# Last MLP of a vision tower on one core: a third result buffer for the left-over tokens, their stores spread, and the rounding of the normalised values moved to GpSimd

## The chip, the cores and the metric

The kernel runs as one program on one core of one Trainium2 chip. The metric is the device time of one execution in microseconds. Before the change it was 2389.38 us, the median of three runs (2388.32 to 2389.45).

A core has five engines that run side by side and meet only at semaphores: TensorE (PE in the profile, with PEld for its weight loads), VectorE (DVE), ScalarE (ACT), GpSimd (POOL) and SyncE (SP), which here only issues transfers. Data lie in an on-chip memory of 128 partitions (SBUF); TensorE writes its products to a second one (PSUM).

## What is computed

A small vision transformer on 64 images. Patch embedding gives each image 197 tokens of 192 values; two attention layers and two MLPs follow, each behind a layer norm and with its input added. The change is in the last MLP, which is quantised:

```python
def _L1_ffn_ref(x0, w1, b1, alpha_w1, alpha_a1, w2, b2, alpha_w2, alpha_a2):
    QN, QP = (-8, 7)
    ...
    xq = _quant_act(x0, alpha_a1)        # round(clip(x / mean(alpha), -8, 7))
    wq1 = _quant_w(w1, alpha_w1)
    x1 = jnp.einsum('bsd,hd->bsh', xq, wq1)
    x1 = x1 * alpha_w1 * alpha_a1.mean() + b1
    x1 = jax.nn.gelu(x1, approximate=False)
    x1 = jnp.clip(x1, -10.0, 10.0)
    hq = _quant_act(x1, alpha_a2)
    wq2 = _quant_w(w2, alpha_w2)
    x2 = jnp.einsum('bsh,dh->bsd', hq, wq2)
    x2 = x2 * alpha_w2 * alpha_a2.mean() + b2
    return x2
...
    h = h + _L1_ffn_ref(_layernorm(h, axis=-1), ...)
```

Tokens are 192 wide, the hidden layer 768.

## The kernel before

Four stages follow each other: `embed_attend`, `mlp_0`, `attention_1`, `mlp_1`. The token stream `h` stays in SBUF all the time. Only `mlp_1`, the last, is changed; it takes about the last 205 of 2389 us.

Tokens are held in tiles of 128 rows. Two images (2 x 197 = 394 tokens) fill three tiles of 128 and leave ten tokens over; the ten tokens of all 32 pairs of images are gathered in three further tiles of 120, 120 and 80 rows. `mlp_1` works on groups of four tiles: 96 tiles make 24 groups, and a 25th group of the three left-over tiles is put in the middle, as group 12. A group is 512 tokens wide (the left-over group 320).

For a group g the steps are, with their lines:

- VectorE, `quantise` (line 1611): each tile is normalised from `h` to `z_xn` in float32 (line 1618), then the four tiles are rounded to `z_xq` in bfloat16 by adding and subtracting a large constant, in two instructions (line 1622). It signals `xn_made` and `quantised`.
- TensorE, `turn_x` (line 1745): transposes `z_xq` to PSUM, eight small products; signals `turned`.
- VectorE, `take_turned_x` (line 1628): clips the turned values to -8 and 7 and writes `z_xt`.
- TensorE, `up` (line 1758): six chunks of 128 hidden units, two products each, to four PSUM banks `z_bank_h`.
- ScalarE, `gelu` (line 1715): Gelu of each chunk to one of four buffers `z_act`.
- VectorE, `clip_chunk` (line 1636): limits each chunk in place.
- Rounding of the hidden values to `z_hid`: chunks 1 and 4 on GpSimd (line 1673), the others on ScalarE (line 1705), two chunks behind the Gelu.
- TensorE, `down` (lines 1769 to 1772): per tile eight products to `z_bank_y`.
- VectorE, `finish` (line 1646): scales the products from PSUM to `z_res`. It first waits (from the third group on) until the stores of the group two before, which used the same buffer of two, have landed.
- GpSimd, `add_stream` (line 1664): adds the token stream in place.
- SyncE, `store` (line 1688): stores the pieces of each tile. A pair of images has four such pieces, a group five or six; the left-over group has 32 pieces of ten rows (7.5 KB), since its rows belong to 32 images.

The order of work is written out by hand. Each engine walks through a list of steps by `in_turn`; a number beside a step says how many groups it is ahead of the loop counter. In one round g VectorE limits chunks 0 and 1 of group g+1, scales group g-1, limits chunk 2 of g+1, takes the turned x of g+2, limits chunks 3 to 5 of g+1 and normalises and rounds group g+3. GpSimd rounds chunk 1 of g+1, adds the stream of g-1 and rounds chunk 4 of g+1. TensorE does `up` of g+1, `turn_x` of g+2 and `down` of g.

## Time and profile before

| | us |
|---|---|
| median of three runs | 2389.38 |
| lowest, highest run | 2388.32, 2389.45 |
| the profiled execution, whole time | 2390.77 |
| its span, first to last instruction | 2389.0 |

The mean granted TensorE clock of the profiled execution is 0.988 of full speed. Over the whole span TensorE is busy 90% of the time, VectorE and ScalarE 84% each, GpSimd 72%. The last four of the forty slices of the page are those of the last MLP:

```profile
DVE  5776676888787689999998999989999998986997
ACT  4677776777776499999999999999999999996886
POOL 5777761333332489899989998989999998993544
```

A digit is the busy share of a fortieth of the span (60 us) in tenths. The page shows one execution; its durations are compared with its own span, and the 1.8 us between span and whole time lie outside.

### The profile page before, as it was taken

What the parts mean: (1) busy time and instruction counts of PE and PEld (TensorE: products, weight loads), DVE (VectorE), ACT (ScalarE), POOL (GpSimd) and SP (SyncE); (2) the same over time, 40 slices, a digit from 0 to 9 for tenths busy, and PEclk for the clock granted to TensorE, in tenths of its full rate; (3) what the DMA queues carried; (4) which work ended last, traced back from release to release, by engine and by line L of the source; (5) the groups of instructions that cost most, each with busy time, mean ns of one, the idle gap of its engine ahead of it and who ended that gap; (6) DMA issues with size and microseconds to landing.
All of it is one profiled execution on the core that took longest, in us unless ns stands there. A gap on an engine that the chain in (4) does not pass through costs nothing. (4 is left out here: it accounts for less than half of the span.)

```text
span 2389.0 us, 76378 instructions
## 1 busy us (share of the span) xinstructions
PE 2161.9 (90%) x25422; PEld 1699.0 (71%) x25422; DVE 1998.4 (84%) x4966; ACT 2008.5 (84%) x5695; POOL 1710.8 (72%) x2215
## 2 busy tenths in 40 slices
PE   5899999999999889999999999999999999988876
PEld 5788885888878567777777777777777777765554
DVE  5776676888787689999998999989999998986997
ACT  4677776777776499999999999999999999996886
POOL 5777761333332489899989998989999998993544
PEclk9999999999999999999999999999999999998999
DMA  6344420000100176666666666666666666673112
GB/s 187 100 115 113 120 71 28 6 5 5 44 15 5 30 124 120 124 121 121 118 125 118 126 118 120 119 124 119 126 119 120 121 122 121 123 120 51 57 48 60
DMA packets 734156, 222.65 MB, mean 93 GB/s; under 512 B 667590, under 2 KB 732720, under 8 KB 733808
## 3 DMA queue, kind: packets, MB, share of 16 engines
q1 hardware_dynamic: 733776, 221.36, 45.5%
q8 instruction: 41, 0.67, 0.1%
q14 instruction: 51, 0.42, 0.1%
q10 hardware_dynamic: 288, 0.20, 0.0%
HBM read 46.49 MB, written 9.68 MB: 24 GB/s over the span
## 5 line engine op out<-in xcount | busy, mean ns | idle before, releaser
L1516 POOL TENSOR_TENSOR b_pr<-b_pr,fc 128x394 f32<-128x394 f32 (+1 forms) x768 | 652.4, 870 | 123.6 <-DVE fc L1436 123.6
L1365 ACT ACTIVATE b_pr<-b_scores,fc 128x197 f32<-128x197 f32 (+1 forms) x1536 | 632.1, 440 | 2.6 <-issue 1.6
L1501 POOL TENSOR_TENSOR b_halves<-b_pr,b_halves 128x394 f16<-128x394 f32 (+1 forms) x640 | 565.3, 909 | 31.5 <-ACT b_halves L1334 27.3
L1273 PE MATMUL b_banks<-fp,wqkv 128*128 128x197 f16 x3840 | 378.8, 249 | 42.4 <-DVE b_qk L1420 38.7
L1430 DVE TENSOR_REDUCE fc<-b_scores 128x2 f32<-128x394 f32 x768 | 395.6, 556 | 4.0 <-PE b_scores L1291 1.9
L1273 PEld LDWEIGHTS b_banks<-fp,wqkv 128*128 128x128 f16 x3840 | 320.8, 98 | 83.7 <-DVE b_qk L1420 61.1
L1334 ACT ACTIVATE b_halves<-b_pr 128x788 f16<-128x788 f32 x384 | 342.6, 892 | 4.9 <-POOL b_pr L1516 4.9
L1365 ACT ACTIVATION_READ_ACCUMULATOR b_pr<-b_scores,fc 128x1 f32 (+1 forms) x1536 | 340.5, 222 | 0.0
L977 POOL TENSOR_TENSOR h<-h,fp_bias 69x192 f32 (+3 forms) x128 | 133.4, 1070 | 266.8 <-DVE m_xn L139 266.8
L1420 DVE SCALAR_TENSOR_TENSOR b_qk<-b_banks,b_qk 128x394 f16<-128x394 f32 x384 | 214.7, 559 | 101.5 <-ACT b_qk L1348 101.3
L1280 PE MATMUL b_banks<-wqkv,fp 128*128 128x384 f16 (+1 forms) x1280 | 254.7, 330 | 40.8 <-DVE h L1455 38.8
L1291 PE MATMUL b_scores<-b_qk 64*128 64x197 f16 (+1 forms) x4608 | 265.3, 248 | 4.6 <-ACT b_pr L1365 4.5
L479 PE MATMUL tokens<-tok_w,parts 128*128 128x192 f16 (+1 forms) x2304 | 212.0, 254 | 49.8 <-POOL parts L338 49.8
L479 PEld LDWEIGHTS tokens<-tok_w,parts 128*128 128x128 f16 (+1 forms) x2304 | 198.2, 109 | 60.0 <-POOL parts L338 39.6
L1291 PEld LDWEIGHTS b_scores<-b_qk 64*128 64x128 f16 (+1 forms) x4608 | 182.8, 103 | 64.6 <-issue 32.0
L338 POOL TENSOR_TENSOR parts<-patches,parts 128x394 f16<-128x394 f32 x192 | 178.9, 961 | 54.0 <-ACT parts L381 53.9
L1280 PEld LDWEIGHTS b_banks<-wqkv,fp 128*128 128x128 f16 (+1 forms) x1280 | 113.9, 105 | 127.2 <-DVE h L1455 53.1
L1348 ACT ACTIVATE b_qk<-b_banks 128x394 f16<-128x394 f32 x384 | 192.2, 519 | 11.1 <-PE b_banks L1273 7.2
L1077 PE MATMUL m_bank_y<-fp,m_hid 128*128 128x192 f16 (+1 forms) x2304 | 195.4, 246 | 1.3 <-DVE h L955 1.3
L1077 PEld LDWEIGHTS m_bank_y<-fp,m_hid 128*128 128x128 f16 (+1 forms) x2304 | 190.4, 105 | 1.7 <-issue 1.5
L1025 ACT ACTIVATE m_act<-m_bank_h,fc_bias 128x394 f32<-128x394 f32 x192 | 112.8, 588 | 87.1 <-PE m_bank_h L1066 75.2
L1066 PE MATMUL m_bank_h<-m_xt,fc 128*128 128x394 f16 x960 | 165.6, 329 | 2.1 <-DVE m_xt L945 2.1
(252 smaller groups left out, 4371.2 us busy)
## 6 DMA issues: line engine op xcount, KB each, us to landing
patches<-in_x SPq DMA_DIRECT2D x64, 588.0 KB, 4.4
b_pt<-b_halves SPq DMA_TRANSPOSE x384, 3.1
out<-z_res SPq DMA_DIRECT2D x62, 96.0 KB
fc<-b_halves SPq DMA_TRANSPOSE x192, 3.2
fp<-b_halves SPq DMA_TRANSPOSE x192, 3.2
m_raw_weights<-in_wqkv SPq DMA_DIRECT2D x2, 1152.0 KB, 6.8
out<-z_res SPq DMA_DIRECT2D x32, 51.8 KB
h<-h SPq DMA_DIRECT2D x32, 44.2 KB
```

What stands on the lines that cost most here:

```text
L479: last = t.matmul(tokens[m][0:ROWS[c], c * D:(c + 1) * D], parts[m][:, pa, k, COLS[c]], tok_w[:, pb, k, :], start=(k == 0 and n == 0), sto ...
L1077: last = t.matmul(bank_y[m][0:ROWS[c], c * D:(c + 1) * D], hid[b][:, pa, f, lo:lo + ROWS[c]], S["fp"][:, pb, f, :], start=(f == 0 and j == ...
L1273: last = t.matmul(out[:, g * SEQ:(g + 1) * SEQ], w[:, (2 * n + g) * P:(2 * n + g + 1) * P], x, start=(j == 0), stop=(j == 4))
L1280: last = t.matmul(out[0:ROWS[c], 0:VH], x[:, COLS[c]], w[:, col:col + VH], start=(j == 0), stop=(j == 4))
L1291: last = t.matmul(scores[n % 2][0:ROWS[c], e, c * SEQ:(c + 1) * SEQ], qk[rows, n, pa, 0, COLS[c]], qk[rows, n, pb, 1, :], start=(j == 0), ...
L1334: return nc.scalar.activation(dst, src, ACT.Copy)
L1348: nc.scalar.activation(qk[:, n, 0], banks[:, k, 0:2 * SEQ].rearrange("p (g t) -> p g t", g=2), ACT.Copy, scale=QK_SCALE).then_inc(qk_hi, 1)
L1365: last = nc.scalar.activation(pr[n % 3][0:ROWS[c], c, e, :], scores[n % 2][0:ROWS[c], e, c * SEQ:(c + 1) * SEQ], ACT.Exp, bias=nmx[n % 2][ ...
L1420: v.scalar_tensor_tensor(out=qk[:, n, 1], in0=banks[:, k, 0:2 * SEQ].rearrange("p (g t) -> p g t", g=2), scalar=QK_SCALE, in1=qk[:, n, 0], ...
L1430: v.reduce_max(nmx[n % 2][:, :, e], scores[n % 2][:, e, 0:2 * SEQ].rearrange("p (c t) -> p c t", c=2), AX.X, negate=True).then_inc(max_mad ...
L1501: nc.gpsimd.tensor_tensor(halves[n % 3][0:ROWS[c], c, 1, :, 0:SEQ], pr[n % 3][0:ROWS[c], c], halves[n % 3][0:ROWS[c], c, 0, :, 0:SEQ], ALU ...
L1516: last = nc.gpsimd.tensor_tensor(p, p, inv, ALU.mult)
```

## The change

- The left-over group (`LEFT`, group 12) gets a third buffer `z_res2` of its own. `finish` and `add_stream` use it for that group, and `finish` of that group waits for no store. The semaphores of the two other buffers no longer count its stores.
- SyncE no longer stores the left-over group at its turn. After the stores of each later group it issues four of the 32 pieces; after eight groups all are out. A wait for them stands before the last waits.
- The rounding to `z_xq` is taken from VectorE and given to GpSimd as a new step `quantise`, the last of its round, for group g+3. It waits for `xn_made` and for the transposes of two groups before, and signals `quantised`. VectorE's own `quantise` now ends with the normalising, and still waits for `quantised` of two groups before.

```diff
@@ -1528,8 +1528,11 @@
     tiles = [(p, k) for p in range(n_img // 2) for k in range(3)]
     groups = [tiles[k:k + GROUP] for k in range(0, len(tiles), GROUP)]
     assert all(len(g) == GROUP for g in groups) and len(rows_left) < GROUP
-    groups.insert(len(groups) // 2, [("left", k) for k in range(len(rows_left))])
+    LEFT = len(groups) // 2
+    groups.insert(LEFT, [("left", k) for k in range(len(rows_left))])
     count = len(groups)
+    LEFT_STORES = 4
+    assert LEFT_STORES * (count - 1 - LEFT) >= n_img // 2
 
     def rows(tile):
         return rows_left[tile[1]] if tile[0] == "left" else P
@@ -1562,7 +1565,7 @@
 
     def stores(last):
 
-        return 16 * sum(len(pieces(tile)) for g in range(last % 2, last + 1, 2) for tile in groups[g])
+        return 16 * sum(len(pieces(tile)) for g in range(last % 2, last + 1, 2) if g != LEFT for tile in groups[g])
 
     with ExitStack() as ctx:
         sb, ps, sem = stage_tools(nc, ctx)
@@ -1572,11 +1575,12 @@
         act_out = [sb(f"z_act{r}", [P, WIDE]) for r in range(4)]
         hid = [sb(f"z_hid{b}", [P, HC, WIDE]) for b in range(2)]
         low_half = [hid[b][:].rearrange("p f t -> p (f t)").bitcast(F16).rearrange("p (f t h) -> p f t h", f=HC, h=2)[:, :, :, 0] for b in range(2)]
-        res = [sb(f"z_res{b}", [P, GROUP, D]) for b in range(2)]
+        res = [sb(f"z_res{b}", [P, GROUP, D]) for b in range(3)]
         bank_x = ps("z_bank_x", [KH, 2, WIDE], BF16)
         bank_h = [ps(f"z_bank_h{r}", [P, 512]) for r in range(4)]
         bank_y = ps("z_bank_y", [P, 2, 512])
         stored = [sem(f"z_stored{b}") for b in range(2)]
+        left_stored = sem("z_left_stored")
         (xn_made, quantised, turned, xt_done, fc_made, gelu_made, clipped, done_by_s, done_by_p, made_y, scaled, h_done, scaled_rstd) = map(sem, (
             "z_xn_made", "z_quantised", "z_turned", "z_xt_done", "z_fc_made", "z_gelu_made", "z_clipped", "z_done_by_s", "z_done_by_p",
             "z_made_y", "z_scaled", "z_h_done", "z_scaled_rstd"))
@@ -1617,10 +1621,6 @@
                         r, j = rows(tile), column(tile)
                         last = v.tensor_scalar(xn[b][0:r, k, :], tokens(tile), mean[0:r, j:j + 1], rstd[0:r, j:j + 1], ALU.subtract, ALU.mult)
                     last.then_inc(xn_made, 1)
-                    dve.wait_ge(xn_made, g + 1)
-                    for lo, hi, r in halves(g):
-                        last = v.tensor_scalar(xq[b][0:r, lo:hi, :], xn[b][0:r, lo:hi, :], ROUND, -ROUND, ALU.add, ALU.add)
-                    last.then_inc(quantised, 1)
 
                 def take_turned_x(g):
                     n = starts(g)[-1]
@@ -1636,9 +1636,9 @@
                     v.tensor_scalar(a, a, S["q_hi"][:, 0:1], S["q_lo"][:, 0:1], ALU.min, ALU.max).then_inc(clipped, 1)
 
                 def finish(g):
-                    b = g % 2
+                    b = 2 if g == LEFT else g % 2
                     dve.wait_ge(made_y, g + 1)
-                    if g >= 2:
+                    if g >= 2 and g != LEFT:
                         dve.wait_ge(stored[b], stores(g - 2))
                     for lo, hi, r in halves(g):
                         scale = S["q2_scale"][0:r, :].unsqueeze(1).to_broadcast([r, hi - lo, D])
@@ -1653,7 +1653,7 @@
                 slots = h[:].rearrange("p i c d -> p (i c) d")
 
                 def add_stream(g):
-                    b = g % 2
+                    b = 2 if g == LEFT else g % 2
                     pool.wait_ge(scaled, g + 1)
                     for lo, hi, r in halves(g):
                         x, at = res[b][0:r, lo:hi, :], [column(tile) for tile in groups[g][lo:hi]]
@@ -1674,20 +1674,34 @@
                                                 ROUND + float(LOW_BITS), ALU.mult, ALU.add).then_inc(done_by_p, 1)
                     return make
 
-                in_turn([(round_chunk(ON_POOL[0]), 1), (add_stream, -1), (round_chunk(ON_POOL[1]), 1)])
+                def quantise(g):
+                    b = g % 2
+                    pool.wait_ge(xn_made, g + 1)
+                    if g >= 2:
+                        pool.wait_ge(turned, g - 1)
+                    for lo, hi, r in halves(g):
+                        last = nc.gpsimd.tensor_scalar(xq[b][0:r, lo:hi, :], xn[b][0:r, lo:hi, :], ROUND, -ROUND, ALU.add, ALU.add)
+                    last.then_inc(quantised, 1)
+
+                in_turn([(round_chunk(ON_POOL[0]), 1), (add_stream, -1), (round_chunk(ON_POOL[1]), 1), (quantise, 3)])
 
             @block.sync
             def _(sp):
+                left = [(k, piece) for k, tile in enumerate(groups[LEFT]) for piece in pieces(tile)]
+
                 def store(g):
-                    b = g % 2
                     sp.wait_ge(h_done, g + 1)
                     for k, tile in enumerate(groups[g]):
                         for i, lo, hi, row in pieces(tile):
-                            if g == count - 1 and k % 2:
+                            if g == LEFT or (g == count - 1 and k % 2):
                                 continue
-                            sp.dma_start(out[i, lo:hi, :], res[b][row:row + hi - lo, k, :]).then_inc(stored[b], 16)
+                            sp.dma_start(out[i, lo:hi, :], res[g % 2][row:row + hi - lo, k, :]).then_inc(stored[g % 2], 16)
+                    if g > LEFT:
+                        for k, (i, lo, hi, row) in left[LEFT_STORES * (g - LEFT - 1):LEFT_STORES * (g - LEFT)]:
+                            sp.dma_start(out[i, lo:hi, :], res[2][row:row + hi - lo, k, :]).then_inc(left_stored, 16)
 
                 in_turn([(store, 0)])
+                sp.wait_ge(left_stored, 16 * len(left))
                 for g in (count - 2, count - 1):
                     sp.wait_ge(stored[g % 2], stores(g))
 
```

## Rows read from the trace of the kernel before

**Rows 1.** Stretches of the last MLP: busy us and (instructions), clock, DMA share, GB/s.

```profile
core 0: us, PE busy (x) PEld busy (x) DVE busy (x) ACT busy (x) POOL busy (x), PEclk, DMA share, GB/s
2206.30:2264.20 57.90, 47.64 (x416) 33.39 (x416) 57.63 (x121) 52.54 (x81) 31.87 (x32) 1.00 0.17 54
...
2298.70:2325.50 26.80, 20.47 (x159) 14.77 (x156) 21.73 (x47) 20.27 (x32) 11.76 (x12) 0.87 0.17 52
```

**Rows 2.** Timeline of VectorE in one group: start us, us, what, count.

```profile
2250.67 0.54 DVE L1636 TENSOR_SCALAR z_act<-z_act,singles 128x512 f32<-128x512 f32 x1
2251.12 0.68 DVE L1628 TENSOR_SCALAR z_xt<-z_bank_x 96x1024 bf16<-96x1024 bf16 x1
2251.73 2.23 DVE L1636 TENSOR_SCALAR z_act<-z_act,singles 128x512 f32<-128x512 f32 x3
2253.88 1.61 DVE L1618 TENSOR_SCALAR z_xn<-h,mean,rstd 128x192 f32<-128x192 f32 x4
2255.53 0.63 DVE L1622 TENSOR_SCALAR z_xq<-z_xn 128x384 bf16<-128x384 f32 x2
2256.07 1.00 DVE L1636 TENSOR_SCALAR z_act<-z_act,singles 128x512 f32<-128x512 f32 x2
2256.99 1.01 DVE L1646 TENSOR_TENSOR z_res<-z_bank_y,q_scale 128x384 f32<-128x384 f32 x2
```

**Rows 3.** Timeline of the other engines in the same group, idle time before in brackets.

```profile
2250.84 2.38 POOL L1664 TENSOR_TENSOR z_res<-h,z_res 128x384 f32<-128x384 f32 x2 [0.23 <-DVE z_res L1646]
2250.90 0.24 PE L1769 MATMUL z_bank_y<-q_sum,base 128*128 128x192 f16 x1 [1.29 <-DVE z_res L1646]
2250.98 0.66 PE L1771 MATMUL z_bank_y<-q,z_hid 128*128 128x192 f16 x6
...
2253.60 0.92 POOL L1673 TENSOR_SCALAR z_hid<-z_act,singles 128x512 f32<-128x512 f32 x1 [0.38 <-DVE z_act L1636]
...
2254.17 1.45 ACT L1715 ACTIVATE z_act<-z_bank_h,q_bias,q_scale 128x512 f32<-128x512 f32 x2 [0.68 <-PE z_bank_h L1758]
...
2256.21 0.65 PE L1745 MATMUL z_bank_x<-ident_b,z_xq 128*96 128x128 bf16 x8
...
2257.16 0.69 POOL L1673 TENSOR_SCALAR z_hid<-z_act,singles 128x512 f32<-128x512 f32 x1 [2.64 <-DVE z_act L1636]
```

**Rows 4.** Single instructions by line: duration ns min/median/max; GpSimd's last addition (timeline).

```profile
L1636 DVE TENSOR_SCALAR z_act<-z_act,singles x2: 636/930/1223, 2251.7 to 2252.3; 128x512 f32<-128x512 f32 x2
L1618 DVE TENSOR_SCALAR z_xn<-h,mean,rstd x1: 751/751/751, 2253.9 to 2253.9; 128x192 f32<-128x192 f32 x1
L1618 DVE TENSOR_SCALAR z_xn<-h,mean,rstd x2: 361/364/367, 2254.6 to 2254.8; 128x192 f32<-128x192 f32 x2
L1673 POOL TENSOR_SCALAR z_hid<-z_act,singles x50: 534/694/958, 2193.4 to 2372.0; 128x512 f32<-128x512 f32 x48, 128x320 f32<-128x320 f32 x2
2377.93 1.94 POOL L1664 TENSOR_TENSOR z_res<-h,z_res 128x384 f32<-128x384 f32 x2 [2.05 <-DVE z_res L1646]
```

**Rows 5.** SyncE's stores behind the left-over group (duration ns), and the stall.

```profile
L1688 SPq DMA_DIRECT2D out<-z_res x35: 289/329/1189, 2294.9 to 2308.9; - x35
2310.42 1.17 PE L1771 MATMUL z_bank_y<-q,z_hid 128*128 128x192 f16 x6
2316.03 1.45 ACT L1715 ACTIVATE z_act<-z_bank_h,q_bias,q_scale 128x512 f32<-128x512 f32 x2 [3.37 <-PE z_bank_h L1758]
2309.14 1.02 DVE L1646 TENSOR_TENSOR z_res<-z_bank_y,q_scale 128x384 f32<-128x384 f32 x2 [3.16 <-DMA out<-z_res]
```

**Rows 6.** Timeline of VectorE, the scaling of groups 0, 8, 13, 16 and 21.

```profile
2206.29 1.01 DVE L1646 TENSOR_TENSOR z_res<-z_bank_y,q_scale 128x384 f32<-128x384 f32 x2
...
2264.22 1.01 DVE L1646 TENSOR_TENSOR z_res<-z_bank_y,q_scale 128x384 f32<-128x384 f32 x2
...
2298.67 1.01 DVE L1646 TENSOR_TENSOR z_res<-z_bank_y,q_scale 128x384 f32<-128x384 f32 x2
...
2325.47 1.01 DVE L1646 TENSOR_TENSOR z_res<-z_bank_y,q_scale 128x384 f32<-128x384 f32 x2
...
2361.69 1.01 DVE L1646 TENSOR_TENSOR z_res<-z_bank_y,q_scale 128x384 f32<-128x384 f32 x2
```

## The prediction, made before the change was timed

> **What bounds the kernel now.** Read the table of stretches first [rows 1]. From 2206.3 to 2264.2 us of the span, inside the last MLP, VectorE (DVE) is busy 57.63 of 57.90 us, ScalarE (ACT) 52.54, GpSimd (POOL) 31.87: VectorE sets the pace and ScalarE is next. Eight groups of four tiles pass here, so ScalarE needs 52.54/8 = 6.57 us a group. The starts of VectorE's scaling (`finish`) give the period: (2264.22 - 2206.29)/8 = 7.24 us [rows 6]. The second row, 2298.7 to 2325.5, is another stage altogether: VectorE is busy only 21.73 of 26.80 us and the granted TensorE clock falls to 0.87. That is the stall behind the left-over group.
>
> Then read one group on VectorE in the timeline [rows 2]. There is no gap between its instructions; each starts some 0.09 us before the record of the one in front ends. The order is the kernel's: limit chunks 0 and 1, scale, limit chunk 2, take the turned x, limit 3, 4 and 5, normalise four tiles, round them (0.63 us for two instructions at L1622). The same group on the other engines [rows 3]: GpSimd works 2.38 us on the addition and 0.92 and 0.69 us on its two roundings; ScalarE waits 0.68 us for TensorE once a group.
>
> Then compare single durations [rows 4]. The same `z_act` instruction takes 0.636, then 1.223 us, where a pair of them that meets nothing takes 1.00 us; the first `z_xn` takes 0.751, the next two 0.36 to 0.37. The slow ones are those that meet GpSimd: `z_act` number two runs against the addition, the first `z_xn` against the rounding at 2253.60. GpSimd in turn needs 0.92 for a rounding that takes 0.69 when VectorE is scaling from PSUM. So VectorE's limiting, normalising and rounding and any GpSimd instruction exclude each other, while scaling and the taking of x (both read PSUM) are not touched. This is the point on which the change turns.
>
> **The left-over group's stores.** Its 120+120+80 rows leave in 32 stores of ten rows. From the end of its addition SyncE issues 35 stores in the 14 us before 2309.15 [rows 5], and the scaling two groups later, in the same buffer, waits 3.16 us for the last of them. ScalarE then stands 3.37 us and TensorE's six matmuls take 1.17 us where 0.66 is normal (granted clock 0.87 over the stretch). Price of it all: from the scaling at 2298.67 to that at 2325.47 three periods pass [rows 6]: 26.80 - 3 x 7.24 = 5.1 us. With a third buffer nobody waits for these stores. What becomes late next? SyncE: after the change a group after the middle issues its own 5 or 6 stores and 4 more, ten of about 0.35 us, 3.5 us in a period of 7. The scaling of a group waits for the stores of two groups before; these start right after their addition and have a whole period and more to land, and the left-over stores stand behind them in the queue, never in front of the same group's. If SyncE needed the 14/35 = 0.4 us for each, ten would still be 4 us. I cost the new stores at nothing and take back all 5.1 us. The eight groups that take four stores each end with group 20, so nothing is added at the end.
>
> **Rounding of x: what VectorE gives away.** Take t = 0 at the end of normalising (2253.88 + 1.61 = 2255.49) [rows 2]. Before: rounding to t = 0.67, chunks 0 and 1 limited by 1.58, scaling 1.50 to 2.51, chunk 2 limited by 2.96 (one period after 2250.67 + 0.54). Without the rounding the limiting starts at -0.09 in place of 0.58: 0.67 us less. Were that all, VectorE would need 6.57 us, exactly what ScalarE needs; nothing below 6.57 is to be had.
>
> **What GpSimd takes on.** Two instructions a group, 128x384 float32 to bfloat16, two constants. The trace has no such one. The nearest is its own TENSOR_SCALAR at L1673: 0.534 us for 320 columns, 0.69 for 512 undisturbed [rows 4, 3]. On the line between them 384 columns take 0.534 + 64 x 0.158/192 = 0.59 us; I call it q and take 0.59. The bounds are the two rows themselves, 0.534 and 0.692; a 16-bit output is not known to cost more. The other bound, far off, is the addition of the same width, 1.94 us for two undisturbed [rows 4], 0.97 each.
>
> Now the collision. GpSimd can start 0.09 us after VectorE ends (2257.07 to 2257.16 [rows 2, 3]), so the first rounding asks at t = 0.1, when the limiting of chunk 0 already runs (-0.09 to 0.45). The rows show what a pair in this order costs: the GpSimd rounding at 2253.60 found chunk 5 running until 2253.96 and ended at 2254.52, 0.56 later, that is its own 0.69 less 0.13; the normalising behind it ended 0.11 after that, and a limiting, 0.17 longer, would end 0.28 after. So:
> chunk 0 limited at 0.45; first rounding ends 0.45 + 0.59 - 0.13 = 0.91; chunk 1 limited 0.91 + 0.28 = 1.19 (0.91 if undisturbed, from 0.45 + 0.46); second rounding ends 1.19 + 0.46 = 1.65; meanwhile VectorE scales from PSUM, undisturbed, 1.10 to 2.12; GpSimd's rounding of chunk 1 follows its second one, to 1.65 + 0.69 = 2.34; chunk 2, ready at 2.03, ends 2.34 + 0.28 = 2.62. Before it ended at 2.96. From there on the order of both engines is as before: the addition starts behind chunk 2 in either kernel. So the period is 7.24 - (2.96 - 2.62) = 6.90 us. In general chunk 2 ends at 0.45 + 2 x (q - 0.13) + 0.28 + 0.69 + 0.28 = 1.44 + 2q, and the period is 5.72 + 2q: 6.79 at q = 0.534, 7.10 at 0.692.
>
> The Trainium skill, SBUF — State Buffer, section Who interferes with whom, says that the pair of ports that VectorE and GpSimd share is an exclusive lock, held for the whole instruction by whoever issues first. By that the order in the sum above (chunk 0, first rounding, chunk 1) follows from the order of issue, as in the trace; the same section wants the conflict put off the critical path, which this change does not do, VectorE being the path.
>
> **Who waits for the moved step.** TensorE's turning needs the second rounding: 1.65 + 0.08 + 0.65 = 2.38. The products `down` behind it start at 2.25 at the earliest anyway (end of scaling plus 0.13); 0.13 us later costs nothing while ScalarE has slack. From the start of `down` to the first Gelu are 2254.17 - 2250.90 = 3.27 us [rows 3]: the Gelu comes at 5.65 in place of 5.92, period 6.90, so ScalarE has 0.33 us left of its 0.68. VectorE takes the turned x at 2.53, after 2.38. GpSimd's new wait for `xn_made` stands in front of the next group's rounding of chunk 1, whose input is there only at 1.19; the wait for `turned` is a period old. GpSimd then has 3.4 + 0.69 + 1.2 us of work in 6.9. All of this is hidden, with 0.15 us as the smallest cover (turning against taking).
>
> **Where it is not hidden.** At the start nothing else runs: 0.09 + 2 x 0.59 in place of 0.63 delays the first turning by 0.6 us. At the end the 0.13 us of `down` may show; 0.2 us. Together 0.8.
>
> **Sum.** The 25 groups are rounded in turn; three in the run-up, one before the first scaling, so 21 periods, 2206.29 to 2361.69 [rows 6], have a moved rounding: 21 x 0.34 = 7.1 us. With the stall 5.1 + 7.1 - 0.8 = 11.4 us. The profiled execution took 2390.8 (span 2389.0 and 1.8 around it), so it would be 2379.4; the median of the runs is 1.4 lower, 2389.4, and gives **2378.0 us**. In formula: 2385.1 + 21 x (period - 7.24).
>
> **Rivals.**
> 1. The roundings hardly meet VectorE (they slip in where it reads PSUM, or the lock is short). For it: conflicts before cost 0.1 to 0.7 us, not always the whole instruction. Against: chunks 0 and 1 stand right behind normalising. Period 6.57 to 6.75: 2371.0 to 2374.8.
> 2. q is longer than the line gives, 0.70 to 0.85 us, or there is one more conflict: period 7.12 to 7.42, 2382.6 to 2388.9. The move alone pays only below q = 0.76 (5.72 + 2q = 7.24); at that point 2385.1, the stall's share alone. For it: 0.92 us is seen for a disturbed 512 columns; against: there the wait is counted in.
> 3. Slower than before: GpSimd's rounding costs as much as its addition of the same width, 0.97 us. Period 7.66, 21 x 0.42 = 8.8 more: 2393.9, and 2395 with the turning then late (0.45 + 0.84 + 0.28 + 0.84 = 2.41, turned at 3.14). It decides from q = 0.86, where 21 periods eat the 4.3 us of stall and start. Against it: 0.69 us for 512 columns of the same operation. The Trainium skill, GPSIMD Engine Reference, section 3.1 Elementwise, speaks for it: for ordinary elementwise work VectorE stays the rule, and two inputs cost 2.6 cycles an element at 1.2 GHz. As an estimate from that page 384 columns would be 0.83 us and the time 2388; its best case of 1.8 cycles gives 0.58, and the row at 512 columns is on the side of the latter.
> 4. The stall does not go (a store in front of the scaling is still late): 2378.0 + 5.1 = 2383.1. Against it the half-empty queue above.
>
> **How the numbers follow.** Forecast 0.52 (own range 2375.7 to 2382.2 from the two rows for q), rival 1 0.15, rival 2 0.20, rival 3 0.07, rival 4 0.06. The range takes the forecast, rival 4, most of rival 2 and the upper part of rival 1: 2372.5 to 2386.5. A difference of 0.2%, 4.8 us, is about what a measurement can tell here: faster is under 2384.6. Faster: 0.52 + 0.15 + 0.06 and a third of rival 2, 0.79; slower 0.06; the rest, 0.15, within.
>
> **What the profile would show.** VectorE: no 0.63 us of `z_xq`; the two `z_act` behind `z_xn` no longer 1.00 but near 1.28 us; scaling every 6.9 us. GpSimd: a new group of 50, mean above 0.6 with its waits. No wait of `z_res` for a DMA, TensorE's clock 1.00 over the middle. ScalarE's wait for `z_bank_h` near 0.3 us. I would be wrong if q is beyond 0.76, if VectorE waits for the turning (a gap in front of `z_xt`), or if scaling too suffers from GpSimd.

## The result

The changed kernel took 2424.84 us (median of four runs, 2420.43 to 2429.58) against 2389.41 us for the kernel before. The ratio is 1.0146, 95% interval 1.0123 to 1.0169: 1.5% slower, where 0.5% faster was forecast. The time lies outside the range and beyond all four rivals.

Page of the profile after, parts 1 and 4 (busy us by engine; the chain that ended last, share of the span):

```profile
PE 2180.9 (90%) x25422; PEld 1712.9 (71%) x25422; DVE 1993.8 (82%) x4916; ACT 2009.2 (83%) x5695; POOL 1789.0 (74%) x2265
...
POOL 6%; issue 2%; DVE 1%; PE 1%; ACT 0%; POOLq 0%; ACTq 0%; DVEq 0%
POOL z_xq L1683 3%; POOL z_res L1664 2%; POOL z_hid L1673 1%; DVE z_xn L1622 0%; DVE z_act L1636 0%; PE z_bank_h L1772 0%; PE z_bank_x L1759 0%; DVE z_xt L1628 0%; PE z_bank_y L1785 0%; ACT z_hid L1719 0%; ACT z_act L1729 0%; POOLq L1606 0%; DVE z_res L1646 0%; DVE rstd L757 0%; PE z_bank_y L1783 0%
```

GpSimd is 78 us busier than in [rows 1]'s kernel as a whole (1710.8 before, 1789.0 now), and it stands first in the chain, with the moved rounding as the largest line. The moved instruction itself, in the view of its line (duration ns min/median/max, 50 of them):

```profile
L1683 POOL TENSOR_SCALAR z_xq<-z_xn x50: 850/1612/2056, 2187.6 to 2388.7; 128x384 bf16<-128x384 f32 x48, 120x384 bf16<-120x384 f32 x1, 80x192 bf16<-80x192 f32 x1
```

A median of 1.61 us. The prediction's q was 0.59 and its bounds 0.53 and 0.69. The 21 periods between the scaling of group 0 and that of group 21, as one stretch of after; the answers to it in before are [rows 1, 6]:

```profile
2212.90:2387.90 175.00, 137.97 (x1083) 99.12 (x1082) 145.46 (x274) 138.63 (x212) 143.68 (x126) 0.91 0.15 47
```

175.0 us in place of 2361.69 - 2206.29 = 155.4, and VectorE (third busy number) now idles 29.5 us of it, where in [rows 1] it had no gap. The whole difference of the two spans, 29.3 us, is made up so: 19.6 in these periods; 7.5 in the run-up (from VectorE's reciprocal of the norm to the first scaling 2212.85 - 2183.74 = 29.1 us, before 2206.29 - 2184.67 = 21.6); 3.1 at the end (2418.3 - 2387.9 against 2389.0 - 2361.7); less 0.9, by which this execution came to the reciprocal earlier.

**Where a group's time goes now.** The chain of waits of after over one group (start us, us, what; "issue" is time without a wait that the profile shows):

```profile
2235.77 3.19 POOL z_xq L1683 x2
2238.96 0.68 POOL z_hid L1673
2239.64 2.11 POOL z_res L1664 x2
2241.74 0.33 issue
2242.07 0.02 POOLq L1681
2242.09 0.04 issue
2242.13 0.91 POOL z_hid L1673
2243.04 1.02 issue
2244.07 0.02 POOLq L1672
2244.08 0.03 issue
```

Every piece of work is GpSimd's: 3.19 for the two roundings of x, 0.68 for chunk 1, 2.11 for the addition, 0.39 until chunk 4 is limited, 0.91 to round it, 1.07 until the normalising is through. That closes in 8.34 us, since the next rounding of x starts at 2244.11, and the next round closes in 8.47, at 2252.58; VectorE's scalings follow in turns of 7.07 and 9.73 us, which is the same mean, 8.40. The 0.39 and 1.07 are waits for VectorE, but VectorE's limiting and normalising there stand behind GpSimd's own instructions ([rows 2 to 4] show the same 0.38 and the first `z_xn` of 0.751), so they belong to the loop. Before, GpSimd had 2.64 us to spare in front of chunk 1 [rows 3]. VectorE and TensorE wait on this loop: TensorE's turning 2.65 us, VectorE's taking 1.45. VectorE and GpSimd thus meet not only at semaphores, as the section on the chip has it: each also lengthens instructions of the other.

```profile
2239.01 0.65 PE L1759 MATMUL z_bank_x<-ident_b,z_xq 128*96 128x128 bf16 x8 [2.65 <-POOL z_xq L1683]
2239.70 0.69 DVE L1628 TENSOR_SCALAR z_xt<-z_bank_x 96x1024 bf16<-96x1024 bf16 x1 [1.45 <-PE z_bank_x L1759]
```

**The run-up.** Stretches of after, four us each from 2188 (columns as in [rows 1]), and the turning of group 0:

```profile
2188.00:2192.00 4.00, 1.20 (x12) 0.68 (x11) 0.65 (x2) 0.00 (x0) 2.61 (x2) 0.99 0.00 0
2192.00:2196.00 4.00, 3.91 (x10) 1.43 (x11) 2.85 (x8) 2.68 (x4) 2.73 (x2) 0.50 0.02 4
...
2190.66 0.65 PE L1759 MATMUL z_bank_x<-ident_b,z_xq 128*96 128x128 bf16 x8 [2.61 <-POOL z_xq L1683]
```

TensorE stands idle for 2.61 us in front of the first turning, and the clock granted falls to 0.50, the lower of its two levels, 1.2 in place of 2.4 GHz, and stays there until about 2208. Before it was 1.00 there; one stretch of that kernel:

```profile
2192.00:2196.00 4.00, 2.80 (x20) 1.43 (x19) 3.79 (x8) 4.00 (x8) 0.70 (x1) 1.00 0.02 4
```

### The profile page after: what moved, and what is told of

Its sections match the earlier page's. It is cut to its first block and busy times, and to the rows that moved or that the text cites. A ratio compares the mean times of both kernels' runs of the same rounds, so it can differ in the third digit from the quotient of the medians.

```text
span 2418.3 us, 76401 instructions
## 1 busy us (share of the span) xinstructions
PE 2180.9 (90%) x25422; PEld 1712.9 (71%) x25422; DVE 1993.8 (82%) x4916; ACT 2009.2 (83%) x5695; POOL 1789.0 (74%) x2265
```

## The experiments

The reasons on trial were these. What makes the moved instruction 1.5 us long (the type written, the operation, or waiting for VectorE)? Is the rest of the prediction's model right once q is? How much is the stores' part worth? How much of the loss is TensorE's clock? The kernel before took 2389 to 2395 us in the different comparisons, so ratios are compared and not medians. The 21 periods are those of one profiled execution each.

| run | ratio to before, 95% interval | 21 periods, us (before 155.4) |
|---|---|---|
| both parts (the change) | 1.0146 (1.0123 to 1.0169) | 175.0 |
| 1, stores only | 0.9986 (0.9977 to 0.9995) | 151.9 |
| 12, stores only, TensorE kept busy | 0.9981 (0.9972 to 0.9990) | 150.2 |
| 2, rounding only | 1.0132 (1.0116 to 1.0147) | 176.7 |
| 3, both, GpSimd writes float32 | 1.0124 (1.0109 to 1.0140) | 175.0 |
| 7, both, TensorE kept busy | 1.0113 (1.0097 to 1.0128) | 173.4 |
| 6, both, step of one addition | 1.0083 (1.0067 to 1.0098) | 167.2 |
| 5, both, multiply by a pointer, add | 0.9991 (0.9981 to 1.0000) | 153.7 |
| 9, both, one pass, multiplier from a pointer | 0.9994 (0.9985 to 1.0003) | 152.7 |
| 8, both, one pass, constants | 0.9952 (0.9939 to 0.9966) | 143.4 |
| 11, the same, TensorE kept busy | 0.9938 (0.9926 to 0.9950) | 142.0 |

Runs 4 and 10 were executed once each, 2435.5 us (with its added stage) and 2383.2 us, and serve for their traces. A pointer in the table is an operand that GpSimd reads from SBUF, one value for each partition, in place of a constant in the instruction.

**1. The stores alone.** The hunks of the change on `LEFT`, `z_res` and `store`, without those on `quantise`.

> Only the stores' part of the change: third buffer for the left-over group, its 32 stores spread, the rounding of x stays on VectorE. Theory of the prediction (the stall is 5.1 us and goes whole): 2384.3 us, 0.2% faster than before, period 7.24 us throughout, no wait of z_res for a DMA. Rival (the spread stores hold something else up, or the stall only moves): 2387 to 2390 us, with a wait of z_res or a longer period in the groups behind the middle.

The wait for a DMA is gone and the periods behind the middle are 7.24 us; the 21 periods are 3.5 us shorter than before, not 5.1. The ratio says 0.14%, 3.3 us, between the 0.2% of the theory and the rival's nothing. The missing part lies just ahead of the left-over group's scaling, in two periods that are 1.6 us longer than without the fall (8.03 and 7.47 us against 6.69 and 7.23 in run 12), where the clock falls (columns as in [rows 1]):

```profile
2276.00:2280.00 4.00, 3.06 (x27) 1.78 (x24) 3.97 (x11) 3.59 (x8) 1.17 (x3) 1.00 0.30 94
2280.00:2284.00 4.00, 3.23 (x23) 3.11 (x24) 4.00 (x9) 2.56 (x5) 3.15 (x4) 0.64 0.04 12
```

The kernel before had 1.00 in the four microseconds from 2280 to 2284 of its own profile. The profiled execution was the slowest of the eleven (2388.66 us, the median is 2386.39), so how often the clock falls there isn't known.

**2. The rounding alone.** The hunks on `quantise` and the order of GpSimd, without the stores.

> Only the rounding of x moved to GpSimd; the left-over stores as before. Theory 1 (all of the loss is the moved rounding, and at a period of 8.4 us the scaling two groups behind the left-over one comes 16.8 us later, after its stores have landed some 14 us behind the addition): about 2425 us, as with both parts, no or hardly any DMA wait of z_res. Rival (the stall adds to it): 2430 us. If the moved rounding were innocent and the stores to blame: 2385 or less.

2420.5 us: the rounding alone carries the loss. I had expected hardly any DMA wait, and there is one of 2.37 us, yet the two periods around it are 17.6 us where two usually are 16.8: the stall costs 0.8 us in so slow a loop.

```profile
2321.49 1.02 DVE L1642 TENSOR_TENSOR z_res<-z_bank_y,q_scale 128x384 f32<-128x384 f32 x2
2330.97 1.02 DVE L1642 TENSOR_TENSOR z_res<-z_bank_y,q_scale 128x384 f32<-128x384 f32 x2 [2.37 <-DMA out<-z_res]
2339.13 1.01 DVE L1642 TENSOR_TENSOR z_res<-z_bank_y,q_scale 128x384 f32<-128x384 f32 x2
```

**3. GpSimd writes float32.**

```diff
-        xq = [sb(f"z_xq{b}", [P, GROUP, D], BF16) for b in range(2)]
+        xr = [sb(f"z_xr{b}", [P, GROUP, D]) for b in range(2)]
+        xq = [xr[b][:].rearrange("p k d -> p (k d)").bitcast(BF16).rearrange("p (k d h) -> p k d h", k=GROUP, h=2)[:, :, :, 1] for b in range(2)]
...
-                        last = nc.gpsimd.tensor_scalar(xq[b][0:r, lo:hi, :], xn[b][0:r, lo:hi, :], ROUND, -ROUND, ALU.add, ALU.add)
+                        last = nc.gpsimd.tensor_scalar(xr[b][0:r, lo:hi, :], xn[b][0:r, lo:hi, :], ROUND, -ROUND, ALU.add, ALU.add)
```

> Both parts of the change, but GpSimd writes the rounded x as float32, and TensorE reads the upper 16 bits of each value, which are the same bfloat16. One thing differs: the type that GpSimd writes. Theory W (the 1.6 us of a rounding is the price of writing 16 bits): a rounding takes 0.6 to 0.65 us, the period is 5.72 + 2q = 6.9 to 7.0 us, the time 2378 to 2380 us. Rival O (the price is that of the operation, two additions of constants, or of its two immediate operands): a rounding still takes 1.5 to 1.6 us and the time is 2420 to 2430 us. Rival L (the price is the waiting for VectorE): the same, 2420 or more.

The median stayed at 1.61 us, the 21 periods at 175.0 and the ratio, 1.0124, within the noise of 1.0146. The type is innocent.

**4. Each form by itself.** Ahead of the last MLP, on tiles that are free then, GpSimd alone, every instruction waited for; three rounds of 13 forms.

```diff
+                for _ in range(3):
+                    then(e.tensor_scalar(o[:, 0:2, :], a[:, 0:2, :], ROUND, -ROUND, ALU.add, ALU.add))
+                    then(e.tensor_scalar(f[:, 0:2, :], a[:, 0:2, :], ROUND, -ROUND, ALU.add, ALU.add))
+                    then(e.tensor_scalar(f[:, 0:2, :], a[:, 0:2, :], s, ROUND, ALU.mult, ALU.add))
+                    then(e.tensor_scalar(o[:, 0:2, :], a[:, 0:2, :], s, ROUND, ALU.mult, ALU.add))
+                    then(e.tensor_scalar(f[:, 0:2, :], a[:, 0:2, :], 2.0, ROUND, ALU.mult, ALU.add))
+                    then(e.tensor_scalar(f[:, 0:2, :], a[:, 0:2, :], ROUND, None, ALU.add))
+                    then(e.tensor_scalar(o[:, 0:2, :], a[:, 0:2, :], ROUND, None, ALU.add))
...
```

> The kernel with the stores' part alone, and before the last MLP a stage in which GpSimd works alone, with all other engines idle: each form of instruction three times, one after another. Theory W: every form that writes bfloat16 (128x384) takes about 1.5 us and every one that writes float32 about 0.6, whatever the operations. Rival O: add and add of two constants takes 1.5 us with either output, multiply by a pointer and add a constant 0.6 with either. Rival L (waiting for VectorE): all forms take 0.6 us, since VectorE is idle. The time of the whole is longer by the stage, 40 to 60 us.

Groups by line, in the order of the diff (L1615 to L1621), then the 512-wide pair L1624 (multiply by pointer, add) and L1625 (add, add); busy us and mean ns of one:

```profile
L1625 POOL TENSOR_SCALAR z_hid<-z_hid 128x512 f32<-128x512 f32 x3 | 5.8, 1932 | 0.2
L1615 POOL TENSOR_SCALAR z_xq<-z_xn 128x384 bf16<-128x384 f32 x3 | 4.5, 1499 | 0.3
L1616 POOL TENSOR_SCALAR z_xn<-z_xn 128x384 f32<-128x384 f32 x3 | 4.5, 1494 | 0.2
L1620 POOL TENSOR_SCALAR z_xn<-z_xn 128x384 f32<-128x384 f32 x3 | 3.5, 1173 | 0.3
L1621 POOL TENSOR_SCALAR z_xq<-z_xn 128x384 bf16<-128x384 f32 x3 | 3.5, 1168 | 0.2
...
L1624 POOL TENSOR_SCALAR z_hid<-z_hid,singles 128x512 f32<-128x512 f32 x3 | 2.1, 692 | 0.3
L1617 POOL TENSOR_SCALAR z_xn<-z_xn,singles 128x384 f32<-128x384 f32 x3 | 1.8, 587 | 0.3
L1618 POOL TENSOR_SCALAR z_xq<-z_xn,singles 128x384 bf16<-128x384 f32 x3 | 1.8, 587 | 0.3
L1619 POOL TENSOR_SCALAR z_xn<-z_xn 128x384 f32<-128x384 f32 x3 | 1.5, 512 | 0.3
```

This settles it for rival O. Add and add takes 1.49 us, with either output; multiply and add takes 0.51 with constants and 0.59 with a pointer; a single addition takes 1.17, twice the pair with a multiplication. The same at 512 columns: 1.93 against 0.69. Nothing else ran, so it isn't waiting; 0.1 us of the 1.61 in the kernel is. Other pairs, an addition of a pointer among them, were not tried, so why an addition in first place is slow stays open.

**5 and 6. The model with other values of q.** The changed kernel with another instruction in GpSimd's step; both leave the rounding of x out.

```diff
+                        last = nc.gpsimd.tensor_scalar(xq[b][0:r, lo:hi, :], xn[b][0:r, lo:hi, :], S["inv_a2"][0:r, 0:1], 0.0, ALU.mult, ALU.add)
```
```diff
+                        last = nc.gpsimd.tensor_scalar(xq[b][0:r, lo:hi, :], xn[b][0:r, lo:hi, :], 1.0, None, ALU.add)
```

> Both parts of the change, but GpSimd's step is a multiplication by a pointer and an addition of zero to bfloat16: it leaves out the rounding, so what is computed afterwards is another thing, of the same size. This is the q of the prediction, 0.587 us alone on the engine. Theory F (the only step that failed is q): two instructions a group of 0.6 to 0.85 us, period 5.72 + 2q = 6.9 us, TensorE's clock 1.00, time 2375.7 to 2382 us. Rival C (the lock costs more or the moved step is late in spite of a short q): period 7.24 or more, 2385 us or more. Rival N (the lock costs less than supposed, as the slow roundings let VectorE through): period 6.6 to 6.75, 2371 to 2375 us.

> Both parts, but GpSimd's step is one addition of a constant to bfloat16, 1.17 us alone (leaves out the rounding). A point between 0.59 and 1.49. Theory F taken literally gives 5.72 + 2 x 1.17 = 8.06 us a group and 2402 us. Rival T (the slow forms hardly hold VectorE up; what costs is that the turning comes late, and TensorE, idle, loses its clock): no loss until the turning is late. The second rounding ends 0.1 + 2.34 = 2.45 us after normalising, turned at 3.2, where VectorE would take it at some 2.4: about 0.8 us more than 6.57, 7.4 us a group and 2388 us if TensorE keeps its clock; 2400 or more, with two kinds of groups, if it does not.

The middle form gave 167.2/21 = 7.96 us a group, in an irregular pattern of 6.8, 7.9 and 9.5 us, with the clock at 0.91 to 0.95: in number near to theory F's 8.06. But that is chance, for the trace shows rival T's mechanism: the pair of limitings behind normalising takes 1.18 us in two of three groups and 1.46 in the third, where theory F would have 1.86 (from -0.09 to 0.45 + 1.04 + 0.28 = 1.77); VectorE waits 1.09 us for the turning in those two; and with the fallen clock there are unequal groups, as its second clause says.

The fast form was a surprise. Its numbers are those of rival C: the clock was 1.00 over the steady groups (it fell to 0.67 from 2280 to 2290 us, beside the left-over group), and yet the period 7.24 us. GpSimd in it (timeline, idle before in brackets):

```profile
2237.12 1.25 POOL L1673 TENSOR_SCALAR z_hid<-z_act,singles 128x512 f32<-128x512 f32 x1 [0.39 <-DVE z_act L1636]
2239.14 1.54 POOL L1683 TENSOR_SCALAR z_xq<-z_xn,singles 128x384 bf16<-128x384 f32 x2 [0.78 <-DVE z_xn L1622]
2240.67 0.85 POOL L1673 TENSOR_SCALAR z_hid<-z_act,singles 128x512 f32<-128x512 f32 x1
2241.49 2.50 POOL L1664 TENSOR_TENSOR z_res<-h,z_res 128x384 f32<-128x384 f32 x2
```

The untouched roundings of chunks 1 and 4 take 0.85 and 1.25 us where 0.69 and 0.92 is usual [rows 3], and the addition 2.50. GpSimd's loop is 7.24 us long again: 1.54 + 0.83 + 2.47 + 0.38 + 1.25 + 0.78. VectorE has no gap in this group either, and its instructions are longer too (see run 9).

**7. TensorE kept busy.** The changed kernel, with transposes of a constant while the rounded x is waited for; the wait for it now stands behind them.

```diff
                     if g:
                         pe.wait_ge(xt_done, g)
+                        for _ in range(30):
+                            t.transpose(bank_x[:, 0, 0:P], S["ident_b"][:, 0:KH], S["ident_b"][:])
```

> The changed kernel, and TensorE does 30 transposes more in each group before it waits for the rounded x, so that it isn't idle there. Theory T (part of the loss is the clock that falls in this wait): granted clock 1.00 from 2212 us on in place of 0.90 to 0.92, no more groups of 9.7 us, every group 7.8 to 8.4 us, time 2400 to 2415 us. Rival (the clock is a side effect, the path is GpSimd): 2420 to 2430 us, or more for the added work.

The stretch of the periods in this kernel:

```profile
2217.00:2390.00 173.00, 156.68 (x1712) 123.61 (x1710) 143.95 (x273) 140.00 (x210) 142.41 (x126) 1.00 0.16 48
```

The clock is 1.00 (0.91 before in this stretch), and every group now takes 8.35 us, where the changed kernel alternates between 7.05 and 9.75. But that is nearly the same mean, and the 21 periods gain 1.6 us in all. Theory T is right on the clock and on the groups (7.8 to 8.4 us), and its time is missed narrowly: the median is 2420.3 us, but beside a kernel before at 2393.9; the ratio 1.0113 makes it 2416.4 beside one at 2389.4, against the theory's 2415. The rival is right on the path, which is GpSimd's loop: the fallen clock mostly shifts time from one group to the next. From VectorE's reciprocal to the end this profile is 3.6 us shorter than that of the changed kernel (2419.4 - 2188.45 = 230.95 against 2418.3 - 2183.74 = 234.56), of some 30 lost. The ratios differ by more, 0.33%, but their intervals overlap. Ahead of the turning of group 0, which has no such filling, the clock fell here too.

**8 and 9. One pass over x.** If multiply and add is the quick form, the rounding can be had from it. Adding a constant c = 12582912 + 17160 in float32 (17160 is hexadecimal 4308) rounds the value to an integer n and leaves hexadecimal 4308 plus n in the lower 16 bits, and read as bfloat16 that is 136 + n for every n from -8 to 7. VectorE limits to 128 and 143, which gives exactly the values of before plus 136, and 136 times the sum of the weights is taken from the bias at the start.

```diff
-                        last = nc.gpsimd.tensor_scalar(xq[b][0:r, lo:hi, :], xn[b][0:r, lo:hi, :], ROUND, -ROUND, ALU.add, ALU.add)
+                        last = nc.gpsimd.tensor_scalar(xr[b][0:r, lo:hi, :], xn[b][0:r, lo:hi, :], 1.0, ROUND + float(X_BITS), ALU.mult, ALU.add)
...
-                    v.tensor_scalar(xt[g % 2][:, :, 0:n], bank_x[:, :, 0:n], 7.0, -8.0, ALU.min, ALU.max).then_inc(xt_done, 1)
+                    v.tensor_scalar(xt[g % 2][:, :, 0:n], bank_x[:, :, 0:n], X_BASE + 7.0, X_BASE - 8.0, ALU.min, ALU.max).then_inc(xt_done, 1)
...
+                        v.tensor_tensor(correction[:], bank_y[:, 0, 0:HC], S["q1_scale"][:], ALU.mult).then_inc(corrected, 1)
+                        dve.wait_ge(corrected, 1)
+                        v.tensor_tensor(S["q1_bias"][:], S["q1_bias"][:], correction[:], ALU.add).then_inc(bias_ready, 1)
...
+                        for f in range(HC):
+                            for k in range(2):
+                                last = t.matmul(bank_y[:, 0, f:f + 1], S["q1"][:, k, f * P:(f + 1) * P], shift_x[:, 0:1], start=(k == 0), stop=(k == 1))
```

> A version with the whole computation: GpSimd multiplies by 1 and adds one constant in float32, so that the lower 16 bits of each sum are the bfloat16 of 136 plus the rounded value; TensorE reads these, VectorE limits to 128 to 143, and 136 times the sums of the weights is taken from the bias once, at the start. Form of instruction: 0.51 us alone. Theory F: period 5.72 + 2 x 0.51 = 6.74 us, 2385.1 - 21 x 0.50 = 2374.6 us, 0.6% faster than before. Rival N (lock cheaper): 6.6 us, 2371.7. Rival C: 7.24 or more, 2385 or more.

Ratio 0.9952, 0.48% or 11.5 us faster than before, where theory F had 0.6%; period 6.78 us, where it had 6.74. One group on VectorE and the rounding on GpSimd:

```profile
2236.43 1.19 DVE L1646 TENSOR_SCALAR z_act<-z_act,singles 128x512 f32<-128x512 f32 x2
2236.60 1.39 POOL L1694 TENSOR_SCALAR z_xr<-z_xn 128x384 f32<-128x384 f32 x2 [1.06 <-DVE z_xn L1627]
2237.54 1.00 DVE L1656 TENSOR_TENSOR z_res<-z_bank_y,q_scale 128x384 f32<-128x384 f32 x2
2238.46 0.53 DVE L1646 TENSOR_SCALAR z_act<-z_act,singles 128x512 f32<-128x512 f32 x1
```

The pair of limitings takes 1.19 us where it took 1.00 [rows 2]: chunk 1 is held up by 0.19 us; scaling and chunk 2 are not. 7.24 - 0.67 + 0.19 = 6.76. VectorE has no gap here, the chain of waits is its own, and the turning is there in time.

Run 9 takes the multiplier of the same kernel from a column of ones:

```diff
-                        last = nc.gpsimd.tensor_scalar(xr[b][0:r, lo:hi, :], xn[b][0:r, lo:hi, :], 1.0, ROUND + float(X_BITS), ALU.mult, ALU.add)
+                        last = nc.gpsimd.tensor_scalar(xr[b][0:r, lo:hi, :], xn[b][0:r, lo:hi, :], one[0:r, 0:1], ROUND + float(X_BITS), ALU.mult, ALU.add)
```

> The one-pass version with one thing changed: the multiplier of GpSimd's step is read from a column of ones in SBUF, as in the fast form measured before, in place of a constant. Alone 0.587 us against 0.51. What made the roundings of chunks 1 and 4 on GpSimd longer in the fast form (0.85 and 1.25 us where 0.69 and 0.92 is usual)? Theory P (two instructions with a pointer one after another, or the pointer's form itself): they are 0.85 and 1.25 again, period 7.2, 2384 to 2386 us for a kernel before at 2389. Rival D (the values that flow through the fast form, which left the rounding out): they stay 0.69 and 0.92, period 5.72 + 2 x 0.587 = 6.9, 2378.

The gain is gone: 0.9994, period 7.25 us. The values are now those of the full computation, and the roundings of chunks 1 and 4 are as slow as in the fast form, so theory P is right (timeline of GpSimd):

```profile
2239.22 1.25 POOL L1687 TENSOR_SCALAR z_hid<-z_act,singles 128x512 f32<-128x512 f32 x1 [0.38 <-DVE z_act L1647]
2241.24 1.55 POOL L1697 TENSOR_SCALAR z_xr<-z_xn,z_one 128x384 f32<-128x384 f32 x2 [0.78 <-DVE z_xn L1628]
2242.77 0.86 POOL L1687 TENSOR_SCALAR z_hid<-z_act,singles 128x512 f32<-128x512 f32 x1
```

VectorE works without a gap here too, and its instructions took longer than in run 8: 1.27 us in place of 1.19 for the pair of limitings, 0.72 in place of 0.53 for chunk 2, 2.41 in place of 2.24 for chunks 3 to 5, 1.65 in place of 1.61 for normalising. These differences add up to 0.48 us, and the period is 0.47 longer. It isn't that the rounding of chunk 4 meets something else: in both runs it starts some 0.35 us before the limiting of chunk 5 ends and then takes 1.25 or 0.91 us.

**10. The counterpart.** The fast form with a constant (0.08) for the pointer; it leaves the rounding out too.

```diff
-                        last = nc.gpsimd.tensor_scalar(xq[b][0:r, lo:hi, :], xn[b][0:r, lo:hi, :], S["inv_a2"][0:r, 0:1], 0.0, ALU.mult, ALU.add)
+                        last = nc.gpsimd.tensor_scalar(xq[b][0:r, lo:hi, :], xn[b][0:r, lo:hi, :], 0.08, 0.0, ALU.mult, ALU.add)
```

> The fast form (no rounding, bfloat16 written) with a constant multiplier in place of the pointer. Theory P: chunk roundings back at 0.69 and 0.92 us, period 6.75 to 6.8. Rival D: still 0.85 and 1.25 us, period 7.1 to 7.2.

0.69 and 0.91 us for the chunks, period 6.82. Runs 5, 8, 9 and 10 are together a two by two, one profiled execution each: the pointer makes the neighbours slow, whatever values are in flight. Why it does is not known. In the run with single forms two pointer instructions in a row took 0.59 each, but all other engines were idle there and each was waited for; it could be the pointer's own read, or how the engine changes between forms. That stays open.

**11. The one-pass version with TensorE kept busy.** Runs 11 and 12 take the transposes of run 7, eight in place of 30, ahead of the same wait: run 11 in the one-pass version, run 12 in that of the stores:

```diff
+                        for _ in range(8):
+                            t.transpose(bank_x[:, 0, 0:P], S["ident_b"][:, 0:KH], S["ident_b"][:])
                     pe.wait_ge(quantised, g + 1)
```

> The one-pass version, and TensorE does 8 transposes more (0.5 us) in each group while it waits for the rounded x. Its idle wait there is 0.74 us. Theory: the granted clock does not fall to 0.57 around group 10 any more, 1 to 1.5 us are won, 0.5 to 0.6% faster than before. Rival: the clock falls all the same, or the added work delays the products, and nothing or less is won: 0.4 to 0.5% faster than before.

Eight transposes a group keep the clock up around the left-over group. The same stretch of the one-pass version without and with them:

```profile
2279.00:2287.00 8.00, 7.46 (x58) 5.66 (x56) 6.27 (x14) 5.00 (x10) 6.34 (x7) 0.81 0.17 42
```
```profile
2279.00:2287.00 8.00, 7.64 (x76) 5.82 (x74) 7.96 (x15) 6.59 (x12) 5.89 (x7) 1.00 0.18 49
```

VectorE is busy 7.96 us in place of 6.27. The 21 periods were 1.4 us shorter (2351.07 - 2209.06 = 142.0), the ratio 0.9938 (0.9926 to 0.9950) against 0.9952 (0.9939 to 0.9966). The intervals overlap, so of the difference between the two versions only the profile speaks; this one has the lowest ratio of all runs, 0.62% faster than before.

**12. The stores, with the clock held.** Run 1 with the same eight transposes.

> The stores' part alone, as in the first experiment, with 8 transposes more a group on TensorE while it waits for the rounded x. There the profiled execution showed TensorE's clock at 0.64 of full between 2280 and 2284 us, beside the left-over group, and lost 1.3 us. Theory (what was missing of the forecast 5.1 us is this clock, and its return at the end): clock 1.00 through the middle, periods of at most 7.24 us there, 0.20 to 0.25% faster than before. Rival (the spread stores give less than the stall costs): 0.14% as before, with the clock high.

The 21 periods are 2353.60 - 2203.36 = 150.24 us, 5.16 less than before. That is the forecast stall to the tenth. The ratio 0.9981 says 4.5 us, but its interval takes in the 0.14% of run 1 too, so it is the periods that decide for the theory. The transposes themselves neither cost nor win anything in these periods: the last MLP of run 4 is that of run 1, without them. In its one profile the clock was not lost, and its 21 periods are 2406.56 - 2256.27 = 150.29 us:

```profile
2256.30:2406.50 150.20, 123.52 (x1082) 86.98 (x1082) 149.48 (x315) 136.43 (x211) 82.59 (x84) 1.00 0.18 55
```

## Why the prediction was wrong

**What bounds the kernel before: right.** VectorE without a gap, period 7.24. Taking 0.67 us from it does shorten the period when the receiver is quick (run 8).

**The left-over group's stores: right.** Priced at 5.1 us, measured at 5.16 in run 12 and 5.11 in the profile of run 4. In run 1 the gain was 3.5 in the periods, since TensorE's clock fell once more. Runs 1 and 4 have the same last MLP, and only run 4 kept its clock there, so the work of the stage alone doesn't decide it. The prediction had not considered the clock; what does decide it stays open. Nothing moved to SyncE, as argued.

**The price of a rounding: here it failed.** The step read "The nearest is its own TENSOR_SCALAR at L1673" and put q on a line between its two widths, 0.59 us, with both rows as bounds. The interpolation in width was good: multiply by pointer and add is 0.587 alone. But the row was of another operation. Multiply and add takes 0.59 us with a pointer; add and add of the same shape and types takes 1.49 us, 2.5 times as much, and 1.61 in the kernel. With this q GpSimd's loop of 8.34 us, and no longer VectorE's work, set the period, where 6.90 was forecast. Run 10 closes the proof: it changes nothing but the operations of this instruction with their constants, and the period falls to 6.82. The prediction said that "a 16-bit output is not known to cost more" and so looked at one difference between the instructions, the type, which was innocent (run 3), and never at the other, the operation. Rival 3 had the right sign and the right mechanism, but stopped at the addition of the same width, 0.97 us, as "the other bound, far off"; the truth was half as far again beyond it. The Trainium skill, GPSIMD Engine Reference, section 3.1 Elementwise, gives 1.8 cycles an element as the best case and 2.6 for two inputs, by which the prediction estimated 0.58 to 0.83 us. The 1.49 us of run 4 is 1.8 times the upper one, and the measurement decides.

**The collision and the formula: the number right at small q, the mechanism wrong at large.** At q = 0.51 the prediction's steps, taken one by one, give chunk 1 at 0.45 + 0.38 + 0.28 = 1.11, scaling to 2.04, chunk 2, no longer held up, at 2.49, and 7.24 - 0.47 = 6.77 us; run 8 had 6.78. (The formula 5.72 + 2q, which I quoted in its expectation, gave 6.74, as it supposes that chunk 2 waits.) At q = 1.49 it gives 8.70; measured were 8.33 to 8.35. There the lock did not behave as the chain supposed. Single instructions of after, chunk 1 limited beside the first rounding (ns):

```profile
L1636 DVE TENSOR_SCALAR z_act<-z_act,singles x1: 720/720/720, 2236.1 to 2236.1; 128x512 f32<-128x512 f32 x1
L1683 POOL TENSOR_SCALAR z_xq<-z_xn x1: 1721/1721/1721, 2235.8 to 2235.8; 128x384 bf16<-128x384 f32 x1
```

The same pair of instructions in the middle form (q = 1.17), then in the one-pass version (q = 0.51):

```profile
L1636 DVE TENSOR_SCALAR z_act<-z_act,singles x1: 726/726/726, 2260.6 to 2260.6; 128x512 f32<-128x512 f32 x1
L1683 POOL TENSOR_SCALAR z_xq<-z_xn x1: 1397/1397/1397, 2260.3 to 2260.3; 128x384 bf16<-128x384 f32 x1
L1646 DVE TENSOR_SCALAR z_act<-z_act,singles x1: 736/736/736, 2236.9 to 2236.9; 128x512 f32<-128x512 f32 x1
L1694 POOL TENSOR_SCALAR z_xr<-z_xn x1: 741/741/741, 2236.6 to 2236.6; 128x384 f32<-128x384 f32 x1
```

In after the limiting starts at 2236.1 and is through at 2236.8, in the midst of a rounding that runs from 2235.8 to 2237.5. It lost 0.18 us, not the rest of the rounding. At q = 1.17 it lost 0.19 us and at q = 0.51 as much, where the chain of the prediction has 0.86 and 0.20. So that the chain gives the right number at q = 0.51 doesn't show that VectorE waited for the whole rounding there, and may be luck. The Trainium skill, SBUF — State Buffer, section Who interferes with whom, has the port pair held for the whole instruction. Of the addition in [rows 3, 4] that is true, of this slow form it is not; what holds in its place stays open. (The advice on the critical path, which the prediction puts in that section of the Trainium skill, stands in the closing Summary of the same text.) So at large q another loop set the period: GpSimd's own work of 6.9 us and two short waits.

That run 8 gains 11.5 us and the forecast was 11.4 is no confirmation of the sum. At its q of 0.51 the formula promises 2389.4 - 2374.6 = 14.8. Of the 21 x 0.46 = 9.7 us that the steady period gives, 8.2 are there with the clock at 1.00 (150.24 - 142.01, runs 12 and 11), since the groups around the left-over one are shorter to begin with; the fallen clock takes 1.4; and the run-up is 1.3 us longer, not 0.5.

**Who waits for the moved step: right in kind.** "VectorE waits for the turning (a gap in front of `z_xt`)" was named as a sign of error, and it is there, 1.45 us. The prediction gave it 0.15 us of cover at q = 0.59; two roundings of 1.6 us pass that by far.

**Run-up and end: mis-sized with q and the clock.** 0.6 us was counted for the start; 7.5 was measured. Of the added time of the first rounding (2.97 us for two in place of 0.63) 2.3 us come at once, and TensorE, idle before, then ran at half its clock for some 16 us. But the chain of waits goes through the roundings of the next groups too (3.53 us for the two of group 2), and the prediction counted only the first. With q = 0.51, 0.59, 1.17 and 1.49 the run-up is 22.9, 24.6, 26.0 and 29.1 us (runs 8, 5, 6 and after), against 21.6. How much of the 7.5 is the clock's isn't shown: in run 7 it was back at 1.00 from 2204 us on, and the run-up was still 28.6, with the added transposes in it. The end was counted at 0.2 and is 3.1 us longer; with the clock held it is 1.6 (2419.4 - 2390.45 = 28.95 us against 27.3). The prediction had taken the clock as given. Over the 21 periods the clock cost 1.6 us (run 7), although the stretch shows it at 0.91 there.

## What to carry to other kernels

- A price is that of an operation with its operand kinds, not of an instruction's name: before work is moved to GpSimd, find or measure a row with the same two operations, since `add, add` cost 2.5 times `mult, add` here, and a pointer in place of a constant cost all that the moved rounding had won.
- When the receiver of moved work is not the bound, add up its whole loop with the new work, its waits included, and ask at which price it becomes the bound; here, as an estimate from the chain of after (8.34 - 3.19 = 5.15), 2q + 5.2 us passes the 7.24 of VectorE from q = 1.0 on.
- Where TensorE waits for another engine's result, read the granted clock behind the wait, in more than one profile: the same last MLP had 0.64 in run 1 and 1.00 in run 4. Eight transposes of a constant in the wait, 0.5 us of otherwise idle time, went with a clock of 1.00 in runs 11 and 12.

## What the runs showed of the hardware that I had not expected

- GpSimd, 128x384, alone: multiply and add of two constants 0.51 us, multiply by a pointer and add 0.59, tensor addition 0.99, one addition of a constant 1.17, two additions 1.49. Writing bfloat16 or float32 makes no difference (at most 5 ns) in the four that were tried with both; multiply and add of two constants was timed alone in float32 only, but takes 1.39 us for two in the kernel with either (runs 8 and 10).
- One form with a pointer in GpSimd's stream beside the others makes unchanged instructions around it longer, on GpSimd 0.69 to 0.85 and 0.92 to 1.25 us, on VectorE chunk 2 from 0.53 to 0.72, while the other engines are at work. Cause open.
- A slow GpSimd instruction of 1.72 us let a limiting on VectorE through with 0.18 us lost, and 0.19 beside one of 1.40 or 0.74 us; the tensor addition held the matching one up until it was through [rows 3, 4].
- TensorE idle for 2.61 us: the granted clock was 0.50 from about 2192 to 2208 us. It fell too beside the small left-over group (0.64 from 2280 to 2284 us in run 1), where the kernel before, and run 4 with the same last MLP as run 1, kept 1.00.
